# Two more drives built by token, dt * u of the third chunk turned earlier, and the last chunk's softplus added by TensorE

## The chip, the cores and the metric

One core of one Trainium2 chip runs the whole program. The metric is the device time of one execution in microseconds (us); the kernel before takes 383.79 us, the median of three runs (382.21 to 384.03).

## The reference, cut to what matters

A Mamba layer (selective scan) over two sequences of 1024 tokens, a layernorm, a mixture of experts with top-2 routing, and a second layernorm. The change lies in the selective scan, for each of 256 channels d, 16 states n and each token t:

```
dt   = softplus(x_conv @ W_dt + b_dt)        # [token, channel]
u    = x_conv
dA   = exp(dt[:, :, None] * A)               # the decay, A = -exp(A_log), one number per state
h    = dA * h + (dt * u)[:, :, None] * B[:, None, :]      # the drive is (dt * u) * B
y    = sum_n h * C
y    = (y + u * D) * silu(z);  out = y @ W_out
```

## The kernel before

**Chunks and units.** The 2048 tokens are cut into four chunks of 512 (`CH`), q = 0 to 3. A unit U = 16 q + n is one state n of one chunk; the 64 units run one after the other. Channels lie on the 128 partitions, in two halves d = 0, 1, and a tile of a unit is 128x1024 (two halves of 512 tokens).

**One unit on the engines.** ScalarE (ACT) writes the decay exp(dt * A_n): for most units as two 128x512 pieces into PSUM (L1078), for a "turned" unit as one 128x1024 piece into `decay_sb` (L1073). VectorE (DVE) runs one scan for each half (`scan`, L1685). GpSimd (POOL) multiplies the state with C (`multiply`, L1443), and TensorE (PE) adds the product into y (`add_to_y`, L682, or L677 in the last chunk).

**The drive (dt * u) * B has two ways.** In the usual one PE spreads row B_n over the partitions (`spread_b`, L649) and DVE multiplies (`drives`, L1656). For a unit in the table `TURNED` ACT multiplies by token: four 128x256 activations with a scale for each token (`drive_by_token`, L1112) on `dtu_t`, the turned dt * u; PE then turns the result back, four 128x128 transposes for each half (`turn_drive`, L668), and DVE's scan reads it from PSUM. DVE has no multiply for such a unit. `drive_beside(U)` says which unit's drive DVE multiplies between the two scans of U.

**What the next chunk needs.** While chunk q runs, the dt of chunk q + 1 is made: ACT takes abs and relu from PSUM, then exp and log (`soften_exp`, `soften_log`), POOL adds the two parts (`finish_dt`, L1461) and multiplies with u (`times_u`, L1473). PE turns that product (`dtu_job`, L720) and ACT copies it into `dtu_t` (`take_dtu`, L1096), before the first turned unit of that chunk.

**The router.** The layer's output for chunk q - 1 is finished beside chunk q: DVE's `gate`, `sort` and `mark`, PE's `project_out` (L774, L776) and `count_choices`, ACT's squares and guess of a root, POOL's `score` (L1484 to L1496) and `add_exps` (to L1504), then DVE's reciprocal (`share`, L1773), POOL's `weigh`.

**What sets the order.** Each engine's queue is written out by hand in a loop over U, and works strictly in that order; semaphores join the engines. Side jobs share two PSUM banks, 0 and 1 in the table `JOBS`: a job may write its bank only when the job before it on this bank has been taken. `TURN`, `OUT`, `SORT`, `RANK`, `SCORE`, `SHARE` say in which unit n of a chunk a step stands.

```
def multiply(U):                       # POOL
    gp.wait_ge(scanned, DT * U + channels.stop)
def scan(U, d):                        # DVE
    if U >= RING:
        dve.wait_ge(product_ready, U - RING + 1)
def share(q):                          # DVE, behind the scans of unit SHARE[q]
    dve.wait_ge(denom_ready, q + 1)
```

## Time and profile before

| | us |
|---|---|
| median of three runs | 383.79 |
| the profiled execution | 382.99 |
| its span on the chip | 381.2 |
| outside the span | 1.8 |
| DVE / PE / POOL / ACT busy | 278.3 / 286.5 / 266.0 / 216.6 |
| chunks q = 2 and 3 (units 32 to 63) | about 141 to 254 |

A row of the timeline reads: start and length in us, engine, line, operation, output from inputs, shape, how many, and in brackets how long the engine stood idle before it and what ended that. Rows merge equal instructions that follow each other. An engine starts its next instruction a little before the last one's length is over: a scan of 1.22 us is followed after about 1.12 us. The unit that a row belongs to follows from counting the scans.

### The profile page before, as it was taken

Reading aid. Unit: us, or ns where it says so; the run is one execution under the profiler, and the core shown is the slowest. Engines: PE = TensorE matmul, PEld = TensorE weight load, DVE = VectorE, ACT = ScalarE, POOL = GpSimd, SP = SyncE. Lnnn points to the kernel's source line nnn. Section 1 sums busy time; section 2 is a strip of 40 time slices with the busy share of each in tenths; the row PEclk is TensorE's granted clock in tenths of the full one; section 3 lists DMA queues with packets and bytes.
Section 4 is the critical chain, followed back from the end, with each engine's and each line's share of the span. In section 5 each row is a group of like instructions: output and inputs, shape, how many; then the busy total and the mean of one; then the engine's idle time right before and its main releaser. Section 6 shows DMA issues by size and latency. Waiting matters only on the chain. (4 is left out here: it accounts for less than half of the span.)

```text
span 381.2 us, 5253 instructions
## 1 busy us (share of the span) xinstructions
PE 286.5 (75%) x1594; PEld 207.8 (55%) x1594; DVE 278.3 (73%) x425; ACT 216.6 (57%) x437; POOL 266.0 (70%) x226
## 2 busy tenths in 40 slices
PE   8797899678877649696465999763389999998700
PEld 6445457446765345486353655332378888887600
DVE  2699889999999799999899899987021333335565
ACT  1858987969964794767757674644003333222305
POOL 4607689977898899999989996995700555556622
PEclk9999999999999987978985899998599999999955
DMA  7061078554343254223112321001153434232773
GB/s 215 24 224 57 2 225 282 156 182 141 102 156 138 83 167 149 70 71 111 56 64 70 131 69 58 0 15 43 51 147 90 121 116 123 82 87 90 217 211 111
DMA packets 35787, 42.91 MB, mean 113 GB/s; under 512 B 3862, under 2 KB 26331, under 8 KB 35760
## 3 DMA queue, kind: packets, MB, share of 16 engines
q1 hardware_dynamic: 32336, 37.38, 32.2%
q0 software_dynamic: 2304, 4.24, 3.4%
q10 hardware_dynamic: 1120, 0.97, 0.9%
q8 instruction: 13, 0.21, 0.2%
q14 instruction: 14, 0.11, 0.1%
HBM read 30.11 MB, written 12.79 MB: 113 GB/s over the span
## 5 line engine op out<-in xcount | busy, mean ns | idle before, releaser
L1443 POOL TENSOR_TENSOR product<-state,c_wide 128x1024 f32<-128x1024 f32 x64 | 149.8, 2346 | 35.3 <-DVE state L1685 23.8
L1078 ACT ACTIVATE psum<-dt,a_neg 128x512 f32<-128x512 f32 x88 | 59.1, 685 | 33.5 <-DVE state L1685 32.3
L682 PE MATMUL psum<-ident,product 128*128 128x128 f32 x384 | 54.7, 290 | 18.8 <-POOL product L1443 18.8
L1685 DVE TENSOR_TENSOR_SCAN state<-psum,drive 128x512 f32<-128x512 f32 x50 | 59.8, 1214 | 4.2 <-ACT psum L1078 3.9
L682 PEld LDWEIGHTS psum<-ident,product 128*128 128x128 f32 x384 | 46.2, 149 | 28.8 <-POOL product L1443 25.7
L1570 POOL DMA_INDIRECT result_rows<-state,result_at x30 | 30.3, 1010 | 40.6 <-DVE state L1899 33.3
L1656 DVE TENSOR_TENSOR drive<-dtu,psum 128x1024 f32<-128x1024 f32 x46 | 55.3, 1201 | 3.8 <-PE psum L649 3.8
L1685 DVE TENSOR_TENSOR_SCAN state<-psum,carry,drive 128x512 f32<-128x512 f32 x42 | 52.8, 1271 | 0.2
L1524 POOL DMA_INDIRECT slot_rows<-sent,scatter_at x32 | 32.8, 1026 | 10.3 <-issue 6.8
L916 PE MATMUL psum<-product,fc_sb 128*128 128x320 f32 x128 | 36.1, 435 | 1.1 <-DVE product L1867 1.1
L1344 ACT ACTIVATE u<-psum 128x640 f32<-128x640 f32 x16 | 11.3, 703 | 38.4 <-PE psum L916 38.4
L1864 DVE TENSOR_SCALAR tags<-c_wide 128x10 f32<-128x10 f32 x8 | 1.3, 164 | 43.2 <-PE psum L905 43.2
L677 PE MATMUL psum<-product,ident 128*128 128x512 f32 x60 | 28.2, 598 | 2.3 <-POOL product L1443 2.3
L916 PEld LDWEIGHTS psum<-product,fc_sb 128*128 128x128 f32 x128 | 22.8, 190 | 11.3 <-ACT z_tok L1344 1.8
L1685 DVE TENSOR_TENSOR_SCAN state<-decay_sb,carry,psum 128x512 f32<-128x512 f32 x22 | 27.0, 1263 | 1.2 <-issue 0.8
L1344 ACT ACTIVATE z_tok<-psum 128x640 f32<-128x640 f32 x16 | 11.3, 703 | 27.6 <-PE psum L916 27.6
L1073 ACT ACTIVATE decay_sb<-dt,a_neg 128x1024 f32<-128x1024 f32 x18 | 20.5, 1140 | 8.8 <-DVE state L1685 8.8
L727 PE MATMUL psum<-x_chan,w_conv 128*128 128x512 f32 x48 | 22.5, 595 | 1.7 <-ACT sent L1185 1.7
L649 PE MATMUL psum<-bc_parts,selector 128*128 128x512 bf16 x46 | 18.2, 399 | 4.3 <-DVE state L1685 3.5
L677 PEld LDWEIGHTS psum<-product,ident 128*128 128x128 f32 x60 | 10.8, 190 | 14.2 <-issue 9.1
L1685 DVE TENSOR_TENSOR_SCAN state<-decay_sb,psum 128x512 f32<-128x512 f32 x14 | 16.4, 1202 | 1.0 <-issue 0.9
L668 PE MATMUL psum<-ident,conv_rows_sb 128*128 128x128 f32 x72 | 11.9, 292 | 6.0 <-DVE drive L1656 3.5
(259 smaller groups left out, 556.1 us busy)
## 6 DMA issues: line engine op xcount, KB each, us to landing
c_wide<-c_rows SPq DMA_DIRECT2D x32, 512.0 KB, 4.2
slot_rows<-blank SPq DMA_DIRECT2D x8, 325.0 KB, 4.9
c_wide<-slot_rows SPq DMA_DIRECT2D x8, 325.0 KB, 3.9
result_rows<-zeros SPq DMA_DIRECT2D x8, 256.0 KB, 5.1
late_rows<-zeros SPq DMA_DIRECT2D x8, 256.0 KB, 4.4
fc_sb<-in_c_fc SPq DMA_DIRECT2D x8, 256.0 KB, 2.9
proj_sb<-in_c_proj SPq DMA_DIRECT2D x8, 256.0 KB, 2.7
c_wide<-result_rows SPq DMA_DIRECT2D x8, 256.0 KB, 5.8
```

The costliest lines, as they stand in the source:

```text
L677: nc.tensor.matmul(psum[:, Y_BANK + d, :], ident[:, :], product[:, i, d, :], start=False, stop=True, skip_group_check=True).then_inc(summe ...
L682: last = nc.tensor.matmul(y_part(j, d), product[:, i, d, j * P:(j + 1) * P], ident[:, :], is_transpose=True, start=False, stop=True, skip_ ...
L727: last = nc.tensor.matmul(psum[:, bank, :], w_conv[:, k, d * P:(d + 1) * P], x_of(q, k), start=(k == 0), stop=(k == D_CONV - 1))
L916: last = nc.tensor.matmul(psum[:, 2 + 2 * (h % 2) + s, 0:HALF], fc_sb[:, i, h * P:(h + 1) * P], rows_chan[:, i, s * HALF:(s + 1) * HALF], ...
L1073: nc.scalar.activation(decay_sb[:, :, :], dt[:, q % 2, :, :], ACT.Exp, scale=a_neg[:, n:n + 1]).then_inc(turned_decay_ready, DT)
L1078: nc.scalar.activation(psum[:, A_BANK + d, :], dt[:, q % 2, d, :], ACT.Exp, scale=a_neg[:, n:n + 1]).then_inc(decay_ready, 1)
L1344: nc.scalar.activation(hidden[e % 2][:, h, :].rearrange("p (s k) -> p s k", s=2), psum[:, 2 + 2 * (h % 2):4 + 2 * (h % 2), 0:HALF], ACT.Ge ...
L1443: nc.gpsimd.tensor_tensor(product[:, U % PRODUCTS, channels, :], state[:, U % RING, channels, :], wide, ALU.mult).then_inc(product_ready, 1)
L1524: gp.indirect_dma_start(out=slot_rows, out_offset=bass.IndirectOffsetOnAxis(ap=scatter_at[:, k, j:j + 1], axis=0), in_=sent[:, k, j, :], i ...
L1570: gp.indirect_dma_start(out=result_rows, out_offset=bass.IndirectOffsetOnAxis(ap=result_at[:, i, s:s + 1], axis=0), in_=rows_out[:, i, s, ...
L1656: nc.vector.tensor_tensor(drive[:, drive_number(U) % 2, :, :], dtu[:, q % 2, :, :], psum[:, b_bank(U), :].unsqueeze(1).to_broadcast([P, DT ...
L1685: nc.vector.tensor_tensor_scan(state[:, U % RING, d, :], decay, rows, before, ALU.mult, ALU.add).then_inc(scanned, 1)
```

## The change

Units 41 (chunk 2, n = 9) and 62 (chunk 3, n = 14) join `TURNED`. The third chunk's dt * u (q = 2) is turned in its units n = 3 and 4, no longer 6 and 7, and with it both halves of y of chunk 1 are turned in n = 5; the banks of these jobs are dealt out anew. For the last chunk `finish_dt` on POOL is gone: PE adds dt and soft with identity matmuls (`sum_dt_job`, n = 10 and 11), ACT copies each half back to `dt` (`finish_last_dt`), POOL's `times_u(3)` waits for both copies and stands in n = 11 and no longer 10. The turning of dt * u of the last chunk moves on PE from n = 12 and 14 to 14 and 15.

```diff
-TURNED = (4, 7, 10, 14, 19, 21, 23, 26, 28, 31, 43, 45, 47, 51, 53, 55, 57, 60)
+TURNED = (4, 7, 10, 14, 19, 21, 23, 26, 28, 31, 41, 43, 45, 47, 51, 53, 55, 57, 60, 62)
-                ("bc3", 1), ("dt3a", 0), ("dt3b", 1), ("y1a", 0), ("y1b", 1), ("t2a", 0), ("t2b", 1), ("out1a", 0), ("out1b", 1), ("rank1", 1),
-                ("t3a", 0), ("t3b", 0), ("y2a", 0), ("y2b", 1), ("out2a", 0), ("out2b", 1), ("z3a", 0), ("rank2", 1), ("z3b", 0),
+                ("bc3", 0), ("dt3a", 1), ("dt3b", 1), ("t2a", 0), ("t2b", 0), ("y1a", 0), ("y1b", 1), ("out1a", 0), ("out1b", 1), ("rank1", 1),
+                ("s3a", 0), ("s3b", 0), ("t3a", 0), ("t3b", 0), ("y2a", 0), ("y2b", 1), ("out2a", 0), ("out2b", 1), ("z3a", 0), ("rank2", 1), ("z3b", 0),
-        TURN = [None, (4, 4), (4, 5), (3, 3)]
+        TURN = [None, (4, 4), (5, 5), (3, 3)]
+            def sum_dt_job(d):
+                q = NQ - 1
+                bank, made = job_bank(f"s{q}{'ab'[d]}")
+                pe.wait_ge(soft_ready, DT * (q + 1))
+                nc.tensor.matmul(psum[:, bank, :], ident[:, :], dt[:, q % 2, d, :], start=True, stop=False)
+                nc.tensor.matmul(psum[:, bank, :], ident[:, :], soft[:, d, :], start=False, stop=True).then_inc(made, 1)
-                if q == 2 and n in (6, 7):
-                    dtu_job(2, n - 6)
-                if q == 2 and n in (12, 14):
-                    dtu_job(3, (n - 12) // 2)
+                if q == 2 and n in (3, 4):
+                    dtu_job(2, n - 3)
+                if q == 2 and n in (10, 11):
+                    sum_dt_job(n - 10)
+                if q == 2 and n in (14, 15):
+                    dtu_job(3, n - 14)
+            def finish_last_dt(d):
+                q = NQ - 1
+                rows, taken = job_made(f"s{q}{'ab'[d]}")
+                nc.scalar.activation(dt[:, q % 2, d, :], rows, ACT.Copy).then_inc(taken, 1)
+                if q == 2 and n in (10, 11):
+                    finish_last_dt(n - 10)
             def times_u(q):
-                gp.wait_ge(dt_ready, DT * (q + 1))
+                if q < NQ - 1:
+                    gp.wait_ge(dt_ready, DT * (q + 1))
+                else:
+                    for d in "ab":
+                        bank, before = JOB[f"s{q}{d}"]
+                        gp.wait_ge(w_taken[bank], before + 1)
-                    elif n == (10 if q == 0 else 6 + q):
+                    elif q < 2 and n == (10, 7)[q]:
                         finish_dt(q + 1)
-                    elif n == (11 if q == 0 else 8 + q):
+                    elif n == (11, 9, 11)[q]:
                         times_u(q + 1)
```

Three places in the engines' queues show it. First PE in units 39 to 41: `product` is y's sum, `selector` a spread of B, `dtu` a turn of dt * u, `w_cat`/`center` the projection of chunk 1's output, `bc_sb` the turn of B, `drive_t` a turned drive. Before:

```order
L682 MATMUL psum<-ident,product 128x128 x8
L649 MATMUL psum<-bc_parts,selector 128x512
L720 MATMUL psum<-ident,dtu 128x128 x4
L774 MATMUL psum<-w_cat,y_chan 128x136 x2
L776 MATMUL psum<-center,x_chan 128x136
L774 MATMUL psum<-w_cat,y_chan 128x136 x2
L776 MATMUL psum<-center,x_chan 128x136
L551 MATMUL psum<-ident,bc_sb 128x16 x4
L682 MATMUL psum<-ident,product 128x128 x8
L649 MATMUL psum<-bc_parts,selector 128x512
```

The same place now (the file's line numbers have moved on by 8 behind L720):

```order
L649 MATMUL psum<-bc_parts,selector 128x512
L782 MATMUL psum<-w_cat,y_chan 128x136 x2
L784 MATMUL psum<-center,x_chan 128x136
L782 MATMUL psum<-w_cat,y_chan 128x136 x2
L784 MATMUL psum<-center,x_chan 128x136
L551 MATMUL psum<-ident,bc_sb 128x16 x4
L682 MATMUL psum<-ident,product 128x128 x8
L668 MATMUL psum<-ident,drive_t 128x128 x4
L782 MATMUL psum<-w_cat,y_chan 128x136 x2
L784 MATMUL psum<-center,x_chan 128x136
```

The turn of dt * u has gone from here. The transposes for unit 41's first half stand behind a projection, the turn of B and a sum; those for its second half stand behind the other projection.

Second ACT in units 42 and 43 (`dt<-psum` is the new copy of a half, `squares` to `rstd1` the layernorm of chunk 1, `decay_sb` the decay of unit 45). Before:

```order
L1086 ACTIVATE carry<-state 128x2
L1112 ACTIVATE conv_rows_sb<-dtu_t,b_t 128x256 x4
L1198 ACTIVATE squares,sum_squares<-sent 128x128 x4
L1204 ACTIVATE log_var1<-sum_squares,epsilon 128x4
L1206 ACTIVATE rstd1<-log_var1 128x4
L1078 ACTIVATE psum<-dt,a_neg 128x512 x2
L1086 ACTIVATE carry<-state 128x2
L1073 ACTIVATE decay_sb<-dt,a_neg 128x1024
```

The same place now:

```order
L1098 ACTIVATE carry<-state 128x2
L1124 ACTIVATE drive_t<-dtu_t,b_t 128x256 x4
L1163 ACTIVATE dt<-psum 128x512
L1215 ACTIVATE squares,sum_squares<-sent 128x128 x4
L1221 ACTIVATE log_var1<-sum_squares,epsilon 128x4
L1223 ACTIVATE rstd1<-log_var1 128x4
L1090 ACTIVATE psum<-dt,a_neg 128x512 x2
L1098 ACTIVATE carry<-state 128x2
L1085 ACTIVATE decay_sb<-dt,a_neg 128x1024
L1163 ACTIVATE dt<-psum 128x512
```

The first copy stands in front of the layernorm's squares, the second behind the decay of unit 45.

Third POOL from unit 37 to the end of unit 43's side jobs. Before:

```order
L1443 TENSOR_TENSOR product<-state,c_wide 128x1024 x4
L1461 TENSOR_TENSOR dt<-dt,soft 128x1024
L1443 TENSOR_TENSOR product<-state,c_wide 128x1024 x2
L1473 TENSOR_TENSOR dtu<-dt,u 128x1024
L1443 TENSOR_TENSOR product<-state,c_wide 128x1024
L1484 TENSOR_SCALAR half_var<-sum_squares 128x4
```

The same place now:

```order
L1462 TENSOR_TENSOR product<-state,c_wide 128x1024 x7
L1497 TENSOR_TENSOR dtu<-dt,u 128x1024
L1508 TENSOR_SCALAR half_var<-sum_squares 128x4
L1510 TENSOR_TENSOR newton<-rstd 128x4
L1511 TENSOR_TENSOR newton<-newton,half_var 128x4
```

The addition is gone, and the multiplication with u stands behind the product of unit 43, directly ahead of `score`.

## Rows read from the trace of the kernel before

**Rows 1.** The page, busy time of each engine (share of the span) and instructions.

```profile
PE 286.5 (75%) x1594; PEld 207.8 (55%) x1594; DVE 278.3 (73%) x425; ACT 216.6 (57%) x437; POOL 266.0 (70%) x226
```

**Rows 2.** Windows, chunk q = 2: length, busy PE, PEld, DVE, ACT, POOL, clock, DMA.

```profile
141.50:197.40 55.90, 41.83 (x243) 32.74 (x243) 52.03 (x70) 38.22 (x89) 51.09 (x39) 0.83 0.29 90
```

**Rows 3.** Timeline, DVE, units 39, 41, 44 and 45.

```profile
164.79 1.22 DVE L1656 TENSOR_TENSOR drive<-dtu,psum 128x1024 f32<-128x1024 f32 x1 [0.71 <-PE psum L649]
...
171.86 1.20 DVE L1656 TENSOR_TENSOR drive<-dtu,psum 128x1024 f32<-128x1024 f32 x1
172.97 1.22 DVE L1685 TENSOR_TENSOR_SCAN state<-psum,drive 128x512 f32<-128x512 f32 x1
...
183.00 1.22 DVE L1685 TENSOR_TENSOR_SCAN state<-psum,drive 128x512 f32<-128x512 f32 x1 [0.88 <-ACT psum L1078]
...
191.53 0.18 DVE L1773 RECIPROCAL denom<-denom 128x4 f32<-128x4 f32 x1 [1.71 <-POOL denom L1504]
```

**Rows 4.** Timeline, POOL, from finish_dt of the last chunk to unit 44's product.

```profile
173.29 2.35 POOL L1461 TENSOR_TENSOR dt<-dt,soft 128x1024 f32<-128x1024 f32 x1
...
178.90 2.36 POOL L1443 TENSOR_TENSOR product<-state,c_wide 128x1024 f32<-128x1024 f32 x1 [0.95 <-issue]
181.22 2.36 POOL L1473 TENSOR_TENSOR dtu<-dt,u 128x1024 f32<-128x1024 f32 x1
183.54 2.36 POOL L1443 TENSOR_TENSOR product<-state,c_wide 128x1024 f32<-128x1024 f32 x1
185.98 0.20 POOL L1484 TENSOR_SCALAR half_var<-sum_squares 128x4 f32<-128x4 f32 x1
...
188.43 2.35 POOL L1443 TENSOR_TENSOR product<-state,c_wide 128x1024 f32<-128x1024 f32 x1
```

**Rows 5.** Timeline, ACT, units 39 to 45.

```profile
166.62 1.31 ACT L1078 ACTIVATE psum<-dt,a_neg 128x512 f32<-128x512 f32 x2
...
178.94 1.71 ACT L1112 ACTIVATE conv_rows_sb<-dtu_t,b_t 128x256 f32<-128x256 f32 x4
180.56 0.29 ACT L1198 ACTIVATE squares<-sent 128x128 f32<-128x128 f32 x1
...
183.61 1.13 ACT L1073 ACTIVATE decay_sb<-dt,a_neg 128x1024 f32<-128x1024 f32 x1
...
192.15 0.57 ACT L1096 ACTIVATE dtu_t<-psum 128x512 f32<-128x512 f32 x1
```

**Rows 6.** Timeline, PE, units 38 to 42, and one product of chunk 3.

```profile
162.36 1.97 PE L682 MATMUL psum<-ident,product 128*128 128x128 f32 x8 [3.34 <-POOL product L1443]
...
165.93 1.94 PE L682 MATMUL psum<-ident,product 128*128 128x128 f32 x8 [0.32 <-POOL product L1443]
...
168.36 0.63 PE L774 MATMUL psum<-w_cat,y_chan 128*128 128x136 f32 x4
...
170.19 1.09 PE L682 MATMUL psum<-ident,product 128*128 128x128 f32 x8
...
174.69 0.60 PE L668 MATMUL psum<-ident,drive_t 128*128 128x128 f32 x4
...
215.98 1.88 PE L677 MATMUL psum<-product,ident 128*128 128x512 f32 x4
```

**Rows 7.** Windows of PE alone: length, busy, clock (1 is full), DMA.

```profile
165.90:167.60 1.70, 1.67 (x8) 0.50 0.36 94
167.70:171.00 3.30, 3.30 (x29) 1.00 0.38 118
```

**Rows 8.** Timeline, all engines, end of the scan.

```profile
250.25 3.63 DVE L1685 TENSOR_TENSOR_SCAN state<-psum,carry,drive 128x512 f32<-128x512 f32 x3
...
251.75 3.57 POOL L1443 TENSOR_TENSOR product<-state,c_wide 128x1024 f32<-128x1024 f32 x2
253.97 1.90 DVE L1842 TENSOR_TENSOR product<-state,c_wide 128x512 f32<-128x512 f32 x1
...
254.03 1.16 PE L790 MATMUL psum<-center,x_chan 128*128 128x136 f32 x8 [1.45 <-DVE state L1685]
```

More of the change, by code:

```diff
@@ L1055, in decays @@
                 for d in range(DT):
-                    if n <= 1:
+                    if n <= 1 and q < NQ - 1:
                         act.wait_ge(dt_ready, DT * q + d + 1)
+                    elif n <= 1:
+                        job_taken(f"s{q}{'ab'[d]}")
                     if U == 0:
@@ L1257, in _ @@
                         drive_by_token(T)
-                if q == 2 and n in (6, 7):
-                    take_dtu(2, n - 6)
-                if q == 2 and n in (13, 15):
-                    take_dtu(3, (n - 13) // 2)
+                if q == 2 and n in (3, 4):
+                    take_dtu(2, n - 3)
+                if q == 2 and n in (10, 11):
+                    finish_last_dt(n - 10)
+                if q == 2 and n in (14, 15):
+                    take_dtu(3, n - 14)
                 if U in PAUSES:
```

## The prediction

> **What bounds the kernel now.** I read the page first: no engine is busy much over 75% of the span [rows 1], because the scan stage and the expert stage have different limits. So I asked for the stretch that the change touches. In chunk 2, DVE is busy 52.03 of 55.90 us and POOL 51.09, ACT only 38.22 and PE 41.83 [rows 2]. DVE works through a fixed order and is the pace; POOL follows each unit's second scan closely. Then I read DVE's timeline for what is not work. Three stalls matter: 0.71 us ahead of the drive of unit 40, where PE's spread of B comes late, 0.88 us ahead of unit 44, where ACT's decay comes late, and 1.71 us ahead of the reciprocal of `share`, where POOL's sum of exponentials comes late [rows 3]. The last is the largest, and it is the end of a chain through POOL: product of unit 42, `times_u`, product of 43, `score`, product of 44, exponentials [rows 4]. Anything in front of `score` on POOL is paid for at 191.53. What follows chunk 2 (chunk 3, the router's tail, the experts) starts from there and moves with it.
>
> **The drive of unit 62.** DVE loses one multiply, 1.11 us from 171.86 to 172.97 [rows 3], so the last scans end 1.1 us earlier. The extra work of ACT, four activations of together 1.71 us [rows 5], falls in unit 59, and PE's transposes in 61 and 62; both have room. At the end PE waits 1.45 us for the last scan and starts at 254.03 [rows 8]. It would start at 252.9. Its first two steps take 1.0 and 1.7 us, and the second needs POOL's product of unit 62, done at 251.75 + 2.3 = 254.05, against the 253.9 at which PE would ask for it. So PE gains 254.03 + 1.0 - 254.1 = 0.9. DVE's own last product takes 1.90 us [rows 8], where POOL's two products run beside it; it may start 1.1 us earlier, or again end only behind POOL's, at 255.87, where PE wants it at 255.8. I take **-0.9**; with the latter it would be -0.85.
>
> The Trainium skill (SBUF — State Buffer, "Who interferes with whom") says that a VectorE operation with two SBUF inputs and a GpSimd operation that reads SBUF exclude each other for the whole instruction. The row agrees: 1.90 us, and an end 0.55 behind POOL's. By that rule the second end, 255.87, is the likelier one.
>
> **The drive of unit 41.** Again 1.11 us of DVE go. But the turned drive must be there in its place. ACT can do it: at 163.7 it has the four activations (1.6 us) and then both copies of y, so it is at unit 40's decay at 166.3, and was at 166.62 [rows 5]; -0.3. PE is the question. It is held until POOL's product of unit 37 at 165.93 [rows 6]. Behind that come the sum and the spread, then, without the four `dtu` transposes (0.44), the first projection at 167.9, which was at 168.36. Projection and turn of B take 1.83 us (168.36 to 170.19), the sum of unit 38 0.93, four transposes 0.60 [rows 6]: ready at **171.3**. DVE wants it at 170.4: unit 40's decay ready at 167.0, then scan, multiply, scan, 3 x 1.12. The second half stands behind another projection, 1.38, and 0.6: ready at 173.1, so the scan that was at 172.97 [rows 3] starts at 173.1. The multiply's 1.11 us are gone and nothing is won: **+0.2** with the clock as it was.
>
> The clock is not likely to stay as it was. PE's granted clock is 0.50 at 165.9 to 167.6 and 1.00 from 167.7 [rows 7]: it had idled 3.34 us before 162.36, and full speed came 5.3 us after work resumed. Now the `dtu` transposes at 164.55 are gone from the place between the two sums and the delayed dt job and both y turns fill 157 to 160. So PE has two gaps, 160.1 to 162.4 and 163.7 (or 164.5) to 165.9, with one sum and one spread between. If the clock is low behind the second gap, it may rise only 5.3 us after 165.93, at 171.2. The 3.4 us of work between 168.1 and the first turned half then take (171.2 - 168.1) / 2 = 1.55 longer: **+1.9** in all. If it never falls, the sum of unit 37 takes 0.9 less, both halves come 1.0 earlier, and unit 41 ends 0.8 before its old time: **-0.8**, less being impossible because of unit 40's decay. Of the ends -0.8 and +1.9, I take **+1.4**, nearer the row of the low clock.
>
> The Trainium skill (TensorE: Matmul & The Clock Gate, "What's actually happening") says that the slow state is the default and that activity releases it. The trace agrees with the rise at 167.65 behind dense work.
>
> **The turns in units 3 and 4.** PE has 0.44 us each more there, ACT 0.48 us each. The bank of dt3a is now that of dt3b, so PE's second dt job waits for ACT's relu, some 1.7 us, until 155.3; the spread for unit 39 is then ready at 159.4 and is wanted at 160.6. Decays 37 and 38 come about 0.1 us before DVE wants them. A slip of 0.1 to 0.3 would fall into the 0.71 us stall of unit 40 [rows 3]. **0**; with that cover gone, 0.3.
>
> **Softplus.** POOL loses 2.35 us at 173.29, but it already stood idle 0.95 us behind that, ahead of unit 42's product, for the scan of unit 42 [rows 4]: removed work before 178.90 only lengthens an idle. What counts is the order behind it. Let everything before be at its old time, unit 42's scan ending at 178.7.
> - POOL: product of 42 ends at 181.2, `times_u` no longer fills the wait for unit 43's scan, which ends at 183.00 - 0.88 = 182.1 [rows 3]. Product of 43 from 182.2 to 184.5.
> - ACT: drive of 45 at 178.94, then the first copy (0.57, pace 0.48), squares and root (180.56 on), decays of 44, carry, decay of 45 from 183.61 + 0.5 = 184.1 to 185.15, then the second copy until **185.75** [rows 5].
> - PE: each sum is two matmuls of 512 columns, 1.88 us at full clock as for one product of chunk 3 [rows 6], 3.6 at half. The second must wait for the first copy, as they share bank 0: 181.2 to 183.1, or 184.8 at half clock. Both are before ACT asks at about 185.2. Behind it wait `count_choices` and the spread for unit 46, ready at 183.9 (or 185.7), wanted at about 184.9; a stall of up to 0.8 is hidden by the longer one below.
> - POOL stands idle from 184.5 to 185.8, then `times_u` 2.32 (181.22 to 183.54), `score` 2.45 (185.98 to 188.43), product of 44 and exponentials 3.10 (188.43 to 191.53) [rows 3, 4]: the reciprocal is at **193.6**, and was at 191.53.
>
> ACT's decay of 44 is 0.5 later too, but DVE has 1.71 us ahead of the reciprocal. So this term is **+2.1**. Bounds: if the copy were there by 184.5, the chain would be 1.25 shorter, +0.8; if the second sum is half a clock late, +2.6. Nothing in chunk 3 absorbs it: POOL's product of 46 waits for unit 46's scan before and after, and from there POOL is back to back.
>
> **Sum.** -0.9 + 1.4 + 0 + 2.1 = +2.6. Against the profiled execution, 382.99, that is 385.6; the median of the three runs is 0.8 above that execution, and gives 386.4. I say 386.0.
>
> **Rivals.** What the measurement can tell from no change is about 0.5%, 1.9 us.
> - *The forecast:* `times_u` waits for ACT, and PE's low clock lasts into unit 41. 386.0, own range 385 to 388. Chance 0.50, slower.
> - *The same wait, but the clock is not worse than before:* -0.9 + 2.1 with -0.8 to +0.2, so +0.4 to +1.4: 383.4 to 385.2. For it: PE is busier ahead of 160 than it was. Against: the second gap. Chance 0.28, no change by measurement.
> - *The second copy is in time:* POOL's chain costs +0.8 and the other terms make it +0.1 to +1.3. About 384. It decides by whether ACT is done with the second copy by 184.5, 1.25 us before my sum. Chance 0.10, no change.
> - *DVE's work counts and POOL's freed time reaches the reciprocal:* two multiplies, 2.2, and the 1.71 us wait gone: -3.9, 379.5. For it: DVE is the busiest engine of the stretch, and POOL has 2.35 us less. Against: POOL idles behind that work already. It decides where POOL starts `times_u`: the reciprocal must come by 189.8. It is faster by more than 1.9 us once at least half of it holds. Chance 0.12.
>
> Faster 0.12, within 0.5% 0.38, slower 0.50. The range leaves out the last rival: from 383.0 (the full clock throughout) to 388.0 (low clock, late second sum, and the median's 0.8).
>
> **What would show it.** In the profile after: POOL idle about 1.3 us ahead of `times_u` with ACT's copy named; DVE waiting 3 us or more for POOL ahead of the reciprocal, against 1.71; DVE waiting for PE's transposes ahead of unit 41's two scans, 0.9 and 0.7 at full clock and more at half; PEclk 0.50 between 168 and 171; the last scan ending 1.1 us nearer to unit 61's. I am wrong if the second copy follows unit 43's product at once, or if the transposes of unit 41 are ready before unit 40's second scan ends.

## The result, and the profile after

The changed kernel takes **387.11 us** (median of four runs, 386.33 to 388.03) against 383.06 for the kernel before on the same chip (four runs, 382.21 to 384.03). The ratio is 1.0104 with an interval of 1.0077 to 1.0132: slower by 1.0%, 4.0 us. The forecast was 386.0, range 383.0 to 388.0, slower as the likeliest case. The profiled execution took 387.78, its span is 386.0, which is 4.8 above the span of before.

The page after, busy time of each engine; it answers to [rows 1]:

```profile
PE 292.3 (76%) x1616; PEld 211.3 (55%) x1616; DVE 277.5 (72%) x423; ACT 220.2 (57%) x445; POOL 264.0 (68%) x225
```

DVE has two instructions and 0.8 us less, POOL 2.0 us less, and the kernel is longer. PE has 5.8 us more. By the lines of the two traces the sums of the softplus are 4.3 of that and the transposes of the two new drives 1.6, less 0.9 for the spreads of B that they need no longer; the rest, 0.8, is the balance of old work that falls into slower or faster stretches of the clock. The same stretch of chunk 2, which answers to [rows 2] (it ends 4.7 us later):

```profile
141.50:202.10 60.60, 45.01 (x258) 34.06 (x258) 51.17 (x69) 40.56 (x94) 49.01 (x38) 0.87 0.25 83
```

DVE and POOL both work less in it than before (51.17 and 49.01 us against 52.03 and 51.09). All of the 4.7 us is waiting. First, the profiled executions reach chunk 2 at slightly different times. DVE's scan at 133.78 before, which is older than all that the change touches, is at 133.89 now, so 0.1 us of every later delay was there at the start. DVE's timeline says where the rest arises; it answers to [rows 3], with the mark of unit 42's end (the copy of `route_values`) and one drive of chunk 3 added. First the two rows of before that these are compared with:

```profile
178.68 0.24 DVE L1728 COPY psum<-route_values 128x96 f32<-128x96 f32 x1
...
213.59 1.22 DVE L1656 TENSOR_TENSOR drive<-dtu,psum 128x1024 f32<-128x1024 f32 x1 [1.03 <-PE psum L649]
```

And after:

```profile
167.09 1.22 DVE L1709 TENSOR_TENSOR_SCAN state<-psum,drive 128x512 f32<-128x512 f32 x1 [0.66 <-ACT psum L1090]
168.47 1.22 DVE L1680 TENSOR_TENSOR drive<-dtu,psum 128x1024 f32<-128x1024 f32 x1 [0.16 <-PE psum L649]
169.61 1.22 DVE L1709 TENSOR_TENSOR_SCAN state<-psum,drive 128x512 f32<-128x512 f32 x1
173.05 1.22 DVE L1709 TENSOR_TENSOR_SCAN state<-decay_sb,psum 128x512 f32<-128x512 f32 x1 [2.23 <-issue]
174.88 1.22 DVE L1709 TENSOR_TENSOR_SCAN state<-decay_sb,psum 128x512 f32<-128x512 f32 x1 [0.61 <-PE psum L668]
...
180.59 0.24 DVE L1752 COPY psum<-route_values 128x96 f32<-128x96 f32 x1
...
185.39 1.22 DVE L1709 TENSOR_TENSOR_SCAN state<-psum,drive 128x512 f32<-128x512 f32 x1 [1.36 <-ACT psum L1090]
...
196.13 0.18 DVE L1797 RECIPROCAL denom<-denom 128x4 f32<-128x4 f32 x1 [3.94 <-POOL denom L1528]
...
219.28 1.22 DVE L1680 TENSOR_TENSOR drive<-dtu,psum 128x1024 f32<-128x1024 f32 x1 [2.12 <-PE psum L649]
```

The rows at 173.05 and 174.88 are unit 41's two scans, which now read turned drives: 2.23 and 0.61 us of waiting where a multiply of 1.11 stood. The first wait is marked "issue", which names no one; the next view shows that PE's transposes (172.36 + 0.60) end just before it. Unit 42 ends at 180.59, 1.9 us later than before. The reciprocal waits 3.94 us for POOL, against 1.71, and stands 15.54 us behind unit 42's end, against 12.85. And a wait that the forecast did not have, 2.12 us at 219.28, was 1.03 us before.

PE's timeline around units 37 to 41, and the row of chunk 3 that the last wait leads to; it answers to [rows 6]:

```profile
162.47 1.09 PE L682 MATMUL psum<-ident,product 128*128 128x128 f32 x8 [2.12 <-POOL product L1462]
163.40 0.38 PE L649 MATMUL psum<-bc_parts,selector 128*128 128x512 bf16 x1
166.04 1.97 PE L682 MATMUL psum<-ident,product 128*128 128x128 f32 x8 [2.26 <-POOL product L1462]
...
168.23 1.11 PE L782 MATMUL psum<-w_cat,y_chan 128*128 128x136 f32 x4
...
172.36 0.60 PE L668 MATMUL psum<-ident,drive_t 128*128 128x128 f32 x4
...
174.19 0.60 PE L668 MATMUL psum<-ident,drive_t 128*128 128x128 f32 x4
...
215.44 3.59 PE L626 MATMUL psum<-u,diag_d 128*128 128x512 f32 x4
```

And windows of PE alone (length, busy, clock, DMA); they answer to [rows 7]:

```profile
162.00:164.00 2.00, 1.31 (x9) 1.00 0.04 8
164.00:166.00 2.00, 0.00 (x0) 0.56 0.11 33
166.00:168.00 2.00, 1.96 (x9) 0.50 0.46 152
168.00:170.00 2.00, 2.00 (x10) 0.50 0.43 143
170.00:172.00 2.00, 2.00 (x15) 0.73 0.10 20
...
216.00:218.00 2.00, 2.00 (x3) 0.50 0.09 37
218.00:220.00 2.00, 2.00 (x6) 0.78 0.10 33
```

There are two gaps, of 2.12 and 2.26 us, with one sum and one spread between them. In the second the granted clock goes from 2.4 to 1.2 GHz: 0.56 over two microseconds puts the fall at 164.2. It is back at 171.1 (0.73 over 170 to 172). Before, it fell at 160.9 and was back at 167.65. So the low stretch is not longer than it was, 6.9 us against 6.8; it lies 3.4 us later, and that puts it in front of unit 41's transposes. The projection at 168.23 shows the price in one row: 1.11 us, where the same four matmuls took 0.63 at 168.36 [rows 6].

POOL's timeline, which answers to [rows 4]:

```profile
184.16 2.37 POOL L1462 TENSOR_TENSOR product<-state,c_wide 128x1024 f32<-128x1024 f32 x1 [1.00 <-issue]
188.13 2.36 POOL L1497 TENSOR_TENSOR dtu<-dt,u 128x1024 f32<-128x1024 f32 x1 [1.60 <-ACT dt L1163]
190.58 0.20 POOL L1508 TENSOR_SCALAR half_var<-sum_squares 128x4 f32<-128x4 f32 x1
...
193.03 2.35 POOL L1462 TENSOR_TENSOR product<-state,c_wide 128x1024 f32<-128x1024 f32 x1
```

and ACT's, which answers to [rows 5]:

```profile
182.47 0.57 ACT L1163 ACTIVATE dt<-psum 128x512 f32<-128x512 f32 x1
...
186.00 1.14 ACT L1085 ACTIVATE decay_sb<-dt,a_neg 128x1024 f32<-128x1024 f32 x1
187.04 0.57 ACT L1163 ACTIVATE dt<-psum 128x512 f32<-128x512 f32 x1
```

POOL is done with the product of unit 43 at 186.53, the second copy ends at 187.61, and `times_u` starts at 188.13. From there the chain of [rows 4] runs as before: `times_u`, `score`, the product of 44, the exponentials.

Last the end of the scan, all engines, which answers to [rows 8]:

```profile
256.00 2.43 DVE L1709 TENSOR_TENSOR_SCAN state<-psum,carry,drive 128x512 f32<-128x512 f32 x2
...
257.44 3.57 POOL L1462 TENSOR_TENSOR product<-state,c_wide 128x1024 f32<-128x1024 f32 x2
258.52 3.04 DVE L1866 TENSOR_TENSOR product<-state,c_wide 128x512 f32<-128x512 f32 x1
...
258.57 1.17 PE L798 MATMUL psum<-center,x_chan 128*128 128x136 f32 x8 [0.31 <-DVE state L1709]
...
262.85 0.69 DVE L1721 TENSOR_TENSOR z_last<-z_last,psum 128x512 f32<-128x512 f32 x1 [1.29 <-PE psum L694]
```

DVE's product took 1.90 us before. Now it starts earlier against POOL's, takes 3.04 and again ends 0.55 behind POOL's (261.56 and 261.01). DVE's first step on `z_last` was here before:

```profile
257.88 0.69 DVE L1697 TENSOR_TENSOR z_last<-z_last,psum 128x512 f32<-128x512 f32 x1 [2.00 <-PE psum L694]
```

So it is 4.97 later, while the two products of POOL are 5.69 later (257.44 against 251.75): unit 62 gives back 0.7. The whole difference of the spans is there by the end of the scan; the rest is 0.2 shorter than before.

### The profile page after: what moved, and what is told of

It is laid out like the page before. It is cut to its first block and busy times, and to the rows that moved or that the text cites. A ratio compares the mean times of both kernels' runs of the same rounds, so it can differ in the third digit from the quotient of the medians.

```text
span 386.0 us, 5312 instructions
## 1 busy us (share of the span) xinstructions
PE 292.3 (76%) x1616; PEld 211.3 (55%) x1616; DVE 277.5 (72%) x423; ACT 220.2 (57%) x445; POOL 264.0 (68%) x225
## 5 line engine op out<-in xcount | busy, mean ns | idle before, releaser
L1090 ACT ACTIVATE psum<-dt,a_neg 128x512 f32<-128x512 f32 x84 | 56.2, 684 | 32.0 <-DVE state L1709 30.8
L1709 DVE TENSOR_TENSOR_SCAN state<-psum,drive 128x512 f32<-128x512 f32 x48 | 57.4, 1212 | 5.1 <-ACT psum L1090 4.9
L1680 DVE TENSOR_TENSOR drive<-dtu,psum 128x1024 f32<-128x1024 f32 x44 | 52.8, 1200 | 4.4 <-PE psum L649 4.4
L1709 DVE TENSOR_TENSOR_SCAN state<-psum,carry,drive 128x512 f32<-128x512 f32 x40 | 50.3, 1268 | 0.2
L1709 DVE TENSOR_TENSOR_SCAN state<-decay_sb,carry,psum 128x512 f32<-128x512 f32 x24 | 29.4, 1260 | 1.2 <-issue 0.8
L926 PEld LDWEIGHTS psum<-product,fc_sb 128*128 128x128 f32 x128 | 22.8, 190 | 11.3 <-ACT z_tok L1363 1.8
L1085 ACT ACTIVATE decay_sb<-dt,a_neg 128x1024 f32<-128x1024 f32 x20 | 22.8, 1141 | 9.3 <-DVE state L1709 9.3
L1709 DVE TENSOR_TENSOR_SCAN state<-decay_sb,psum 128x512 f32<-128x512 f32 x16 | 18.8, 1203 | 3.8 <-issue 3.2
L649 PE MATMUL psum<-bc_parts,selector 128*128 128x512 bf16 x44 | 17.3, 397 | 3.5 <-DVE state L1709 3.0
L1124 ACT ACTIVATE conv_rows_sb<-dtu_t,b_t 128x256 f32<-128x256 f32 x40 | 17.0, 496 | 0.0
```

What stands on the lines that cost most here:

```text
L926: last = nc.tensor.matmul(psum[:, 2 + 2 * (h % 2) + s, 0:HALF], fc_sb[:, i, h * P:(h + 1) * P], rows_chan[:, i, s * HALF:(s + 1) * HALF], ...
L1085: nc.scalar.activation(decay_sb[:, :, :], dt[:, q % 2, :, :], ACT.Exp, scale=a_neg[:, n:n + 1]).then_inc(turned_decay_ready, DT)
L1090: nc.scalar.activation(psum[:, A_BANK + d, :], dt[:, q % 2, d, :], ACT.Exp, scale=a_neg[:, n:n + 1]).then_inc(decay_ready, 1)
L1680: nc.vector.tensor_tensor(drive[:, drive_number(U) % 2, :, :], dtu[:, q % 2, :, :], psum[:, b_bank(U), :].unsqueeze(1).to_broadcast([P, DT ...
L1709: nc.vector.tensor_tensor_scan(state[:, U % RING, d, :], decay, rows, before, ALU.mult, ALU.add).then_inc(scanned, 1)
```

## The experiments

**Theory.** Three waits, each with its own cause: (1) unit 41's transposes are late because PE's clock is low after two gaps, (2) the reciprocal is late because `times_u` waits for ACT's second copy directly ahead of `score`, (3) PE's clock in chunk 3 rises later, and the spread of B for drive 53 (`spread_b`, L649) with it. Against them stands the gain of unit 62. **Rivals.** That the loss is all in one part, and the other harmless; that PE simply has too much work in these stretches, whatever its clock; that POOL's chain is late because units 41 and 42 are late, not because of the copy.

Each ratio below is against the kernel before on the same chip, whose medians were 383.83 us beside the first four kernels (21 runs), 383.87 beside the next four (25) and 384.23 beside the last two (12); a hundredth of the ratio is 3.8 us. The ratio is the one on record, with its interval of 95%; it is not the quotient of the two medians, and the two differ by up to 0.0015. A difference between two of these kernels is taken from their ratios, and is uncertain by some 1.3 us. Each kernel has one profiled execution. They reach chunk 2 at different times, so a distance inside one profile is safer than a time of day: against the kernel before, the scan at 133.78 is 0.6 earlier in experiment 1, 0.5 in 3 and 0.3 in 4. "Unit 42's end" is the row of `route_values`, "drive 53" the multiply that stands at 213.59 before and 219.28 after.

**1. The softplus alone, on the kernel before.** The units, the turns of chunk 2's dt * u and the y turns stay as they were. (The two new functions, the end of `finish_dt` for the last chunk and the waits are as in the change, and left out here.)

```diff
-                ("t3a", 0), ("t3b", 0), ...
+                ("s3a", 0), ("s3b", 0), ("t3a", 0), ("t3b", 0), ...
+                if q == 2 and n in (10, 11):
+                    sum_dt_job(n - 10)
-                if q == 2 and n in (12, 14):
-                    dtu_job(3, (n - 12) // 2)
+                if q == 2 and n in (14, 15):
+                    dtu_job(3, n - 14)
+                if q == 2 and n in (10, 11):
+                    finish_last_dt(n - 10)
-                    elif n == (11 if q == 0 else 8 + q):
+                    elif n == (11, 9, 11)[q]:
                         times_u(q + 1)
```

> The kernel before with one part of the change: the last chunk's softplus summed by TensorE and copied by ScalarE, times_u(3) in unit 43. Units 41 and 62 keep their multiply, dt * u of chunk 2 is turned in n = 6 and 7. Theory (POOL's chain through times_u waits for the second copy): +2.5 to +2.9 us on before, the reciprocal of share in chunk 2 some 2.7 us later, DVE idle ahead of it about 4 us. Rival (the loss of the change comes from the turned drive of unit 41 and PE's clock alone): within 0.5 us of before.

Measured 386.98 us (386.55 to 388.21), ratio 1.0097 (1.0070 to 1.0123): +3.7 us. POOL and DVE in its timeline:

```profile
185.46 2.36 POOL L1497 TENSOR_TENSOR dtu<-dt,u 128x1024 f32<-128x1024 f32 x1 [1.61 <-ACT dt L1163]
```

```profile
193.44 0.18 DVE L1797 RECIPROCAL denom<-denom 128x4 f32<-128x4 f32 x1 [3.92 <-POOL denom L1528]
```

Unit 42 ends at 177.91 here, 0.8 earlier than before, of which 0.6 was there at the start, and still POOL idles 1.61 us for the copy and the reciprocal comes 15.53 us behind unit 42, as in the changed kernel. So wait (2) is not handed on from unit 41: the softplus makes it alone. The time is 0.8 to 1.2 above the expectation (its upper end, 2.9, lies just inside the interval of 2.7 to 4.7). Drive 53 waits 2.31 us here, against 1.03 before, which is wait (3), with unit 41 left out of it; the expectation had no such term.

**2. Unit 62 alone, on the kernel before.**

```diff
-TURNED = (4, ..., 43, 45, 47, 51, 53, 55, 57, 60)
+TURNED = (4, ..., 43, 45, 47, 51, 53, 55, 57, 60, 62)
```

> The kernel before with unit 62 alone added to TURNED. Theory: -0.9 us (0.7 to 1.0), the last scan 1.1 us earlier, and DVE's last product still ending only behind POOL's last one. Rival (the end is bound by POOL, as its products do not move): 0.

Measured 382.84 us (381.79 to 384.75, 12 runs), ratio 0.9988 (0.9968 to 1.0008): -0.45 us with an interval from -1.2 to +0.3. One row of DVE:

```profile
252.60 3.04 DVE L1842 TENSOR_TENSOR product<-state,c_wide 128x512 f32<-128x512 f32 x1
```

The second step on `z_last` is at 257.79, against 258.74: 0.95 earlier in the profile. Unit 42 ends 0.2 earlier already, so unit 62 gives 0.7 here too. The whole span is only 0.2 shorter, because the part behind the scan took 0.75 longer, and that part varies: from `z_last` to the end it lasted between 122.3 and 123.6 us in the twelve profiled executions. The mechanism shows; the size in the time is too small for this measurement.

**3. Unit 41 alone.** The changed kernel without unit 62 and with the softplus on POOL as before; the early turns of dt * u and the new banks, which unit 41 needs, are in.

```diff
-TURNED = (4, ..., 31, 41, 43, 45, 47, 51, 53, 55, 57, 60, 62)
+TURNED = (4, ..., 31, 41, 43, 45, 47, 51, 53, 55, 57, 60)
-                if q == 2 and n in (10, 11):
-                    sum_dt_job(n - 10)
-                    elif n == (11, 9, 11)[q]:
+                    elif n == (11 if q == 0 else 8 + q):
                         times_u(q + 1)
...
```

(The rest of the softplus is taken back in the same way.)

> The kernel before with unit 41 added to TURNED and dt * u of chunk 2 turned in n = 3 and 4, softplus as before on POOL, unit 62 as before. Theory (PE brings the turned drive late behind two projections, at half clock): +1.0 to +2.0 us, DVE waiting 2 us and 0.6 us ahead of unit 41's scans. Rival (the multiply taken from DVE is a gain): -1.1 us.

Measured 385.74 us (384.62 to 387.38), ratio 1.0060 (1.0035 to 1.0085): +2.3 us. Its two scans of unit 41:

```profile
171.94 1.22 DVE L1698 TENSOR_TENSOR_SCAN state<-decay_sb,psum 128x512 f32<-128x512 f32 x1 [0.97 <-issue]
173.77 1.22 DVE L1698 TENSOR_TENSOR_SCAN state<-decay_sb,psum 128x512 f32<-128x512 f32 x1 [0.61 <-PE psum L668]
```

The low clock here lasts from about 166.5 to 169.9, and the first wait is 0.97, not 2.23 and not the 2 of the expectation. Unit 42 ends at 179.49, +0.8, and +1.3 with the 0.5 that this profile was ahead at the start. But 0.8 of that are two waits that neither the kernel before nor the change has, 0.38 us ahead of DVE's drive at 153.85 and 0.45 ahead of its scan at 156.66. The granted clock was half from about 149.4 to 152.8 here; in the other two kernels it was half from 140.4 to 147.2, though PE does the same work in the same order up to that point. So where the low stretches fall can differ with the same work ahead of them, and a wait that hangs on them may be of another size in another execution; one profile for each kernel cannot tell. The reciprocal waits 1.70 us, as before the change. Drive 53 is 1.5 late, of which 0.7 is its own longer wait (1.75). So with POOL's softplus in place wait (2) is absent, and waits (1) and (3) are there. The time, +2.3 with an interval from 1.3 to 3.3, lies above the expected 1.0 to 2.0. Both parts of the change lose by themselves; the rival that one of them is harmless is out.

**4. The clock held in chunk 2.** The changed kernel, but the four transposes of each half of y are done four times over (the same result written again), and the second half's turn moves to unit n = 6, so that PE has something to do in both gaps.

```diff
-        TURN = [None, (4, 4), (5, 5), (3, 3)]
+        TURN = [None, (4, 4), (5, 6), (3, 3)]
-                for j in range(TPC):
+                for j in [j for _ in range(4 if q == 1 else 1) for j in range(TPC)]:
-                        if n == TURN[q][d] + 1:
+                        if n == (6 if q == 2 else TURN[q][d] + 1):
```

> The changed kernel, with TensorE's two gaps of units 37 to 39 filled: the turn of y's first half (n = 5) and that of its second half (now in n = 6) are each done four times over, same data to the same bank. Theory (the half clock from 164.6 to 171 is what makes unit 41's drive later than I computed for full clock): the granted clock stays 1.0 from 160 to 172, the wait ahead of unit 41's first scan goes from 2.2 us to under 0.3, and the kernel is 2 us (1.3 to 2.6) faster than the changed one, so +1.5 to +2.7 on before. Rival (the order on PE alone, two projections ahead of the transposes, makes the wait): less than 0.5 us faster than the changed one.

Measured 385.25 us (383.43 to 386.74), ratio 1.0041 (1.0015 to 1.0067). Against the change's 1.0104 that is 2.4 us less, for more work on PE. Its windows of PE, and DVE at unit 41:

```profile
164.00:166.00 2.00, 1.49 (x15) 1.00 0.00 0
166.00:168.00 2.00, 2.00 (x19) 1.00 0.67 205
```

```profile
170.21 1.22 DVE L1709 TENSOR_TENSOR_SCAN state<-decay_sb,psum 128x512 f32<-128x512 f32 x1
172.04 1.22 DVE L1709 TENSOR_TENSOR_SCAN state<-decay_sb,psum 128x512 f32<-128x512 f32 x1 [0.61 <-PE psum L668]
...
177.75 0.24 DVE L1752 COPY psum<-route_values 128x96 f32<-128x96 f32 x1
```

The clock is 1.00 from 158 to 174, the wait of 2.23 is gone, and unit 42 ends 2.84 us earlier than in the change, 0.9 earlier than before it. Some of that was there at the start: counted from the scan at 133.78 on, it is 2.4 earlier than in the change and 0.6 earlier than before it. Drive 53's wait is shorter too, 1.52 and not 2.12, so the 2.4 us of the time are not all wait (1). More transposes made PE's chain faster, so "PE has too much work" is out for wait (1). What is left, 0.61, is a place in the queue: a projection of 1.39 us stands between the two halves at full clock, here (169.96 to 171.35) and in the change (172.80 to 174.19). The reciprocal stays 15.54 us behind unit 42: wait (2) is untouched.

**5. The copies earlier.** The changed kernel, both sums in n = 10, the first copy ahead of ACT's drive of unit 45, the second ahead of the squares, and `times_u` in n = 10 again.

```diff
-                if q == 2 and n in (10, 11):
-                    sum_dt_job(n - 10)
+                if q == 2 and n == 10:
+                    sum_dt_job(0)
+                    sum_dt_job(1)
+                if q == 2 and n == 10:
+                    finish_last_dt(0)
...
-                if q == 2 and n in (10, 11):
-                    finish_last_dt(n - 10)
+                if q == 2 and n == 10:
+                    finish_last_dt(1)
-                    elif n == (11, 9, 11)[q]:
+                    elif n == (11, 9, 10)[q]:
                         times_u(q + 1)
```

> The changed kernel with the two sums of the last softplus both in unit 42 on TensorE, the first copy ahead of ScalarE's wait for unit 42's scan, the second right behind the turned drive of unit 45, ahead of the layernorm's squares, and times_u(3) behind unit 42's product again. Theory (the second copy's place behind squares and decays makes POOL idle and the reciprocal late): POOL starts times_u within 0.5 us of the end of unit 42's product, the reciprocal comes about 13.3 us after the end of unit 42's second scan, where it came 15.5 us, and the kernel is 2.0 us (1.5 to 2.4) faster than the changed one. Rival (it is the work added on TensorE and ScalarE, not its place): less than 0.5 us faster.

Measured 384.82 us (382.88 to 386.18, 12 runs), ratio 1.0022 (1.0002 to 1.0042): 3.1 us less than the change. POOL and DVE:

```profile
182.99 2.37 POOL L1500 TENSOR_TENSOR dtu<-dt,u 128x1024 f32<-128x1024 f32 x1 [0.16 <-ACT dt L1164]
```

```profile
193.31 0.18 DVE L1800 RECIPROCAL denom<-denom 128x4 f32<-128x4 f32 x1 [1.40 <-POOL denom L1531]
```

`times_u` fills the time in which POOL waits for unit 43's scan, as it did before the change. The reciprocal is 13.05 us behind unit 42's end (180.26), against 15.54. That takes back 2.49 us of wait (2), all but 0.2 of what the change added, although unit 41 is as late as ever. The time fell by more than the expected 1.5 to 2.4; 0.46 of the surplus stands in the profile at drive 53, which waits 1.66 us here, and the rest is within the uncertainty.

**6. The clock brought back early in chunk 3.** The changed kernel, the four transposes of unit 51's first half done five times over.

```diff
-                for j in range(TPC):
+                for j in [j for _ in range(5 if (U, d) == (51, 0) else 1) for j in range(TPC)]:
```

> The changed kernel with the transposes of unit 51's first half done five times over, in a gap of TensorE in chunk 3. Theory (the part of the loss that arises in chunk 3 is the half clock there, under start_y, ahead of the drive of unit 53): the wait ahead of that drive goes from 2.1 us to about 1, the kernel 1.1 us (0.7 to 1.4) faster than the changed one. Rival (the wait comes with the order on TensorE, which is that of before): unchanged, 0.

Measured 385.27 us (384.21 to 386.26, 12 runs), ratio 1.0035 (1.0019 to 1.0050): 2.6 us less than the change. PE and its windows:

```profile
207.82 4.68 PE L668 MATMUL psum<-ident,drive_t 128*128 128x128 f32 x24
...
214.29 1.88 PE L626 MATMUL psum<-u,diag_d 128*128 128x512 f32 x4
```

```profile
210.00:212.00 2.00, 2.00 (x12) 0.58 0.10 33
212.00:214.00 2.00, 1.14 (x11) 1.00 0.07 27
```

Full clock comes at about 211.7 and not at 218.9. The four matmuls of L626 take 1.88 us and not 3.59, and drive 53 does not wait at all. (Those four took 2.50 us before the change, where full clock came at 212.05, in the midst of them.) The waits of chunk 2 are as in the change (2.23, 0.61 and 3.94). So the 2.12 us of waiting in the change, and by the same row the 1.03 in the kernel before, come from the low clock; experiments 8 and 10 take the latter away. The expectation of -1.1 (at most -1.4) was too small: it counted only what the change had added, and the kernel before had the rest to give.

**7. `times_u` one unit earlier, on the kernel before with unit 62.** It tests whether POOL's chain can do better than before.

```diff
+TURNED = (4, ..., 57, 60, 62)
-                    elif n == (11 if q == 0 else 8 + q):
+                    elif n == (11 if q == 0 else 9):
                         times_u(q + 1)
```

> The kernel before with unit 62 in TURNED and times_u(3) one unit earlier, behind unit 41's product, where POOL stood idle; softplus on POOL as before, unit 41 as before. Theory (what stands on POOL between unit 42's scan and score is paid for at the reciprocal): the wait ahead of the reciprocal falls from 1.7 to about 0.7 us, the kernel 1.9 us (1.5 to 2.2) faster than before, 0.9 of it from unit 62. Rival (POOL's order does not count): 0.9 us faster.

Measured 382.41 us (381.50 to 382.90), ratio 0.9953 (0.9934 to 0.9971): -1.8 us, 1.35 of it beyond experiment 2. The reciprocal:

```profile
190.39 0.18 DVE L1773 RECIPROCAL denom<-denom 128x4 f32<-128x4 f32 x1 [0.73 <-POOL denom L1504]
```

It waits 0.73, against 1.71: in the kernel before, POOL's wait can be shortened by order alone. But half of that is lost again in chunk 3, at drive 53:

```profile
212.93 1.22 DVE L1656 TENSOR_TENSOR drive<-dtu,psum 128x1024 f32<-128x1024 f32 x1 [1.51 <-PE psum L649]
```

The reciprocal is 1.14 earlier than before, yet full clock comes at 211.9 and so only 0.15 earlier, and the wait of 1.03 has grown to 1.51. Nothing that PE does up to this point was moved. So the rise of the clock does not move with DVE, and wait (3) is not a thing of the change alone.

**8. The fills of 4 and 6 and the order of 7, on the kernel before.** Unit 62 is in. The fill of chunk 2 here is the second half of y, eight times over.

```diff
-                for j in range(TPC):
+                for j in [j for _ in range(5 if (U, d) == (51, 0) else 1) for j in range(TPC)]:
-                for j in range(TPC):
+                for j in [j for _ in range(8 if (q, d) == (1, 1) else 1) for j in range(TPC)]:
```

> The kernel of the run before this one, with y's second half of chunk 1 turned eight times over in n = 5 (over the gap at 159 to 162 us) and unit 51's first transposes five times. Theory (half clock ahead of the drives of units 40 and 53 makes the waits there, 0.7 and 0.2 and 1.0 us): granted clock 1.0 from 160 to 168, those waits down to 0.3 and 0.2, 1.0 to 1.5 us on top, 3.1 us faster than before. Rival (ScalarE's copies, which wait for the same gap, take the place of the wait): no more than 1.9 us faster than before.

Measured **380.16 us** (379.16 to 380.95), ratio 0.9903 (0.9879 to 0.9927): 3.7 us faster than the kernel before. The windows of PE show 1.00 from 158 to 174 and from 208 to 220, drives 40 and 53 do not wait, and unit 42 ends at 177.81. The expectation was -3.1.

**9. The change with all three mended** (4, 5 and 6 together; their diffs are above).

> The whole change with its three losses mended: copies early as in the run with both sums in unit 42, TensorE's gaps of units 37 to 39 filled by y turns done four times, unit 51's first transposes five times. Theory (the terms add): from the changed kernel -2.2 (POOL's order), -2.4 (clock ahead of unit 41), -1.5 (clock in chunk 3), so about 2 us (1.5 to 2.7) faster than before, and 1 to 2 us behind the kernel that keeps unit 41's multiply and POOL's softplus with the fills. Rival (the terms hide one another): 0 to 1 us faster than before.

Measured **380.69 us** (379.65 to 382.19), ratio 0.9906 (0.9887 to 0.9924). It is 3.6 us faster than the kernel before, where 1.5 to 2.7 was expected. From 1.0104 that is 7.6 us, where the three gave 2.4, 3.1 and 2.6 one by one, 8.1 together: they add up to within the measurement, though the first two hold some of wait (3) as well. Its profiled execution, 382.19, is the longest of its six (the others are 379.65 to 381.05), and in it the third wait is not gone:

```profile
213.43 1.22 DVE L1683 TENSOR_TENSOR drive<-dtu,psum 128x1024 f32<-128x1024 f32 x1 [1.18 <-PE psum L649]
```

The twenty transposes for unit 51 ran at full clock here, the clock fell behind them, at 208.6, and was back only at 212.1. So this fill does not hold the clock in every execution, and how often it does is not known.

**10. The two fills of 8 alone, on the kernel before.** No drive is added and no order changed: only transposes that write the same result again.

> The kernel before with the two fills alone (y's second half of chunk 1 turned eight times in n = 5, unit 51's first transposes five times). Theory: waits of 0.9 and 1.0 us ahead of units 40 and 53 gone, 1.9 us (1.4 to 2.3) faster than before. Rival (the fills pay only beside the other edits): under 1 us.

Measured 380.88 us (379.83 to 384.02), ratio 0.9921 (0.9894 to 0.9948): -3.0 us, with an interval from -4.1 to -2.0. The expectation was -1.9 (at most -2.3). In the profile `z_last` gains 2.1, counted from the scan at 133.78, which is what the waits give that are gone or shorter; what the rest of the 3.0 is, if it is real, is open. So most of what 8 and 9 win comes from the fills. The mended change (0.9906) is neither measurably better nor worse than the kernel before with two fills (0.9921): the intervals overlap. That is what shows that the waits (1) to (3) make up the change's loss: with them mended, and the same kind of fill on both sides, no loss is left that exceeds the uncertainty of 1.3 us and the 0.7 that unit 62 gives the change.

## Why the prediction was right, point by point

It was right in direction, and 387.11 lies inside the range. The signs that it named are in the profile: POOL idle ahead of `times_u` for ACT's copy, DVE waiting over 3 us ahead of the reciprocal, half clock from 168 to 171. The sum was +2.6 and the time went up 4.0 (span 4.8), so in size it was short by a third or more, and that 387.11 still lies in the range is in part luck: the upper end, 388.0, allowed for a second sum that comes late on PE. It was not late (183.09 to 185.1, and ACT took it at 187.04); that room was filled by other things, chunk 3 above all. The terms, in the profiles:

| term | forecast | measured | what shows it |
|---|---|---|---|
| unit 62 | -0.9 | -0.7 | POOL's last products 5.69 later, `z_last` 4.97; experiment 2, the same |
| unit 41 | +1.4 | +1.8 | unit 42's end, 178.68 to 180.59, less the 0.1 at the start; experiment 4 takes 2.4 of it away |
| turns in n = 3 and 4 | 0 | 0 | DVE's drive at 153.91 before stands at 154.02, but the 0.11 is already there at 133.78; the 0.71 ahead of unit 40's drive is gone, 0.66 ahead of unit 40's scan took its place |
| softplus, `share` | +2.1 | +2.7 | unit 42 to reciprocal, 12.85 to 15.54; experiments 1 and 5 |
| chunk 3 | none | +1.1 | drive 53's wait, 1.03 to 2.12; experiment 6 |

**Unit 41.** The low-clock case was computed as +1.9 with full speed at 171.2; it came at 171.1 and the term was 1.8. The full-clock case was computed as -0.8; experiment 4, which holds the clock, has -0.6, counted from the scan at 133.78 (-0.9 as it stands). The two ends were about right and the value taken between them, +1.4, was hedged. Experiment 3 lies between (+1.3, or +0.5 without the two waits at 153.85 and 156.66), with a shorter low stretch, so the clock, and not the place in the queue, sets most of this term. The place is worth the 0.61 that stays.

**Softplus.** The second copy was forecast to end 7.05 us behind unit 42's end (185.75 - 178.7) and ended 7.02 behind (187.61 - 180.59). Product of 44 and exponentials took 3.10 as reckoned. What was missed: POOL began 0.52 us after the copy's end, where the sum had 0, and `times_u` to the next product took 4.90 (188.13 to 193.03) where the sum had 4.77. POOL's idle time, forecast at 1.3, is 1.60. That POOL's saved 2.35 us does not reach the end was right too; the rival that ends on the faster side is refuted by the reciprocal at 196.13.

**Unit 62.** DVE's last product ends behind POOL's, the second of the two cases given: moved back by 5.69, 261.56 is the 255.87 of the forecast. PE's last sum begins 0.10 behind it (261.66) and its matmuls and the step to DVE take a little longer than reckoned, so -0.7 and not -0.85. The Trainium skill (SBUF — State Buffer, "Who interferes with whom") says that a VectorE operation with two SBUF inputs and a GpSimd operation that reads SBUF shut each other out. The trace agrees: DVE's product takes 3.04 us now and 1.90 before, it starts 1.1 us earlier against POOL's, and it ends the same 0.55 behind POOL's end, in experiment 2 as well.

**Chunk 3: the step that failed.** The prediction said that what follows chunk 2 "starts from there and moves with it". It did not quite: drive 53 waits 1.1 us longer, since full clock came 22.8 us behind the reciprocal (218.9 and 196.13) and 20.5 behind it before (212.05 and 191.53). Experiment 1, which leaves unit 41 and the early turns alone, has this wait too (2.31), and experiment 3, which leaves the softplus alone, has some of it (1.75). Experiments 5 and 7 have 1.66 and 1.51, and 7 has neither the softplus nor unit 41 of the change. That the wait is the clock's is shown by experiment 6. What makes the clock rise later in one profile than in another, a moved piece of work or nothing of the program's, was not tried and stays open; the 1.1 us is the size in this one execution.

With the measured sizes the sum is -0.7 + 1.8 + 0 + 2.7 + 1.1 = 4.9, and with the 0.1 at the start it is the delay of `z_last`, 4.97; the spans differ by 4.8.

## What to carry to other kernels

Work taken from a busy engine pays only if the work that takes its place is ready where the old work ended: here a multiply of 1.11 us gave way to waits of 2.84, and an addition of 2.35 us on POOL to a wait for ACT directly ahead of the chain that DVE needs. Ask of each moved step what stood idle beside it, and put the new step into that idle time (experiment 5), not behind it. And when PE is the one that is late, look at its granted clock before its work: filling two short gaps with transposes whose result is not needed was worth 3.0 us of 384 (2.0 to 4.1) with nothing else changed, 2.1 of it seen in the profile. Last, before a delay in one profile is put down to an edit, look where the two profiles stood before anything that was edited: here that was 0.1 to 0.6 us, as much as some of the terms.

## What was not expected of the hardware

- Behind a gap of 2.12 us on PE and 1.3 us of work, the granted clock went from 2.4 to 1.2 GHz 0.4 us into a second gap, of 2.26 us, and it stayed there for 6.9 us (164.2 to 171.1), 5.0 of them full of work. In experiment 3, with gaps of 0.92 and 2.26, it fell only at 166.5, 1.1 us after the work had resumed. Transposes held it at 1.00 in experiment 4 and were PE's only work from 207.8 to 212.5 in experiment 6, where it rose at 211.7. Where the low stretches fall does not seem to be fixed by the program's work alone: up to 149 us experiment 3 does the same work as the kernel before, in the same order, and was at half clock from 149.4 to 152.8 where that was at half clock from 140.4 to 147.2.
- POOL's start behind ACT's copy took 0.52 us when POOL had been idle (1.60 us, `times_u` at 188.13). In experiment 5, where POOL came to its wait just as the copy ended (182.77), it started after 0.22. Experiment 1 has 0.53, again with POOL idle. Why is open.
- The rise of the clock in chunk 3 did not move with the work of the other engines: in experiment 7 DVE is 1.1 us ahead and the rise 0.15, and DVE waits 0.5 us longer for PE.
